# An attention batch on four engines: where the output projection stands on TensorE, and where ScalarE makes queries and keys

## What is computed

```python
qkv = (x @ Wqkv.T + bqkv).reshape(Bb, Ss, 3, H, HD).transpose(2, 0, 3, 1, 4)
attn = jax.nn.softmax(jnp.einsum('bhid,bhjd->bhij', q, k) / jnp.sqrt(jnp.float32(HD)), axis=-1)
coh = jax.nn.sigmoid(jnp.tanh(comb @ Wc1.T + bc1) @ Wc2.T + bc2).transpose(0, 2, 1)
mod = attn * coh[..., None]
mod = mod / (mod.sum(-1, keepdims=True) + 1e-08)
mod = (1.0 - fi) * mod + fi * fa[:, None, :, None]
out = jnp.einsum('bhij,bhjd->bhid', mod, v).transpose(0, 2, 1, 3).reshape(Bb, Ss, Ee)
return out @ Wout.T + bout
```

## Time and profile before

| | us |
|---|---|
| median of 3 runs | 784.82 |
| the three runs | 787.23, 784.77, 784.82 |
| the profiled execution, its own time | 787.02 |
| its span | 785.2 |
| PE busy in the span | 741.9 |
| ACT busy | 575.6 |
| DVE busy | 557.1 |
| POOL busy | 312.2 |

### The profile page before, as it was taken

How to read it: one execution, slowest core, us unless ns; L and a number is a source line. 1 busy time by engine, 2 the same in 40 slices (tenths; PEclk the granted TensorE clock), 3 DMA queues, 4 the chain that set the end, 5 groups by cost and what they waited for, 6 DMA issues and landing times.

```text
span 785.2 us, 14852 instructions
## 1 busy us (share of the span) xinstructions
PE 741.9 (94%) x5314; PEld 654.1 (83%) x5314; DVE 557.1 (71%) x1495; ACT 575.6 (73%) x1001; POOL 312.2 (40%) x214
## 2 busy tenths in 40 slices
PE   6889998979878999999999999999999999999998
PEld 4666767869766799899989989999898899999887
DVE  4887888477379877976977797688679756833422
ACT  3677777369797778978987886897889788553243
POOL 2122222179977175344717543572645161000000
PEclk9999999989997999999999999999999999999999
DMA  8940000000000000000000000000000000000000
GB/s 313 333 117 2 3 1 2 1 1 1 1 1 1 1 1 8 2 1 2 7 1 2 8 1 1 1 8 1 1 5 4 1 1 8 1 1 8 1 1 8
DMA packets 11160, 16.92 MB, mean 22 GB/s; under 512 B 680, under 2 KB 6992, under 8 KB 10832
## 3 DMA queue, kind: packets, MB, share of 16 engines
q1 hardware_dynamic: 10944, 15.72, 6.2%
q10 hardware_dynamic: 144, 0.26, 0.1%
HBM read 14.93 MB, written 1.05 MB: 20 GB/s over the span
## 4 chain that ended last, share of the span: by engine, by line
PE 85%; DVE 6%; ACT 4%; issue 3%; DMA 1%; SPq 0%; DVEq 0%; ACTq 0%
PE banks L448 79%; PE banks L484 4%; ACT G_both L936 2%; PE banks L695 2%; DVE W_both L1444 1%; DMA region<-in_pA 1%; ACT region L1014 1%; DVE acc L1589 1%; PE banks L512 1%; DVE W_both L1213 0%; DVE HF L1450 0%; ACT region L1020 0%; PE banks L727 0%; DVE pairs L1408 0%; DVE top_keys L1403 0%
## 5 line engine op out<-in xcount | busy, mean ns | idle before, releaser
L390 POOL TENSOR_TENSOR region<-sim 128x1024 f32<-128x1024 f32 x128 | 260.8, 2065 | 100.1 <-DVE top_keys L1401 63.2
L1076 ACT ACTIVATE HF<-banks,lpack 128x256 f32<-128x256 f32 x256 | 105.4, 479 | 55.6 <-PE banks L448 54.6
L1014 ACT ACTIVATE region<-region,neg_thr 128x1024 f32<-128x1024 f32 x128 | 143.8, 1153 | 0.0
L1444 DVE SCALAR_TENSOR_TENSOR W_both<-region,rz_rel,W_both 128x1024 f32<-128x1024 f32 x98 | 138.1, 1409 | 1.7
L448 PE MATMUL banks<-HF,w_sb 128*128 128x256 f32 x512 | 124.7, 388 | 7.7 <-DVE HF L1450 7.6
L448 PEld LDWEIGHTS banks<-f_sb,HF 128*128 128x128 f32 x1024 | 123.7, 192 | 3.4
L1020 ACT ACTIVATE region<-region,dtop 128x1024 f32<-128x1024 f32 x114 | 125.3, 1141 | 0.0
L448 PE MATMUL banks<-f_sb,HF 128*128 128x128 f32 x1024 | 124.5, 275 | 0.0
L448 PE MATMUL banks<-cT,f_sb 128*128 128x256 f32 x512 | 122.7, 382 | 0.1
L448 PEld LDWEIGHTS banks<-HF,w_sb 128*128 128x128 f32 x512 | 95.4, 194 | 20.0 <-DVE HF L1450 8.6
L448 PEld LDWEIGHTS banks<-cT,f_sb 128*128 128x128 f32 x512 | 92.1, 190 | 16.3 <-issue 2.9
(11 more groups left out here) (167 smaller groups left out, 1032.7 us busy)
## 6 DMA issues: line engine op xcount, KB each, us to landing
w_sb<-in_w SPq DMA_DIRECT2D x1, 2048.0 KB, 14.0
f_sb<-in_f SPq DMA_DIRECT2D x1, 2048.0 KB, 15.8
region<-in_wq SPq DMA_DIRECT2D x1, 1024.0 KB, 7.9
region<-in_wqT SPq DMA_DIRECT2D x1, 1024.0 KB, 10.0
w_sb<-in_w SPq DMA_DIRECT2D x1, 1024.0 KB, 8.5
out_x<-acc_f SPq DMA_DIRECT2D x16, 64.0 KB, 1.6
x1T_all<-in_xT SPq DMA_DIRECT2D x1, 768.0 KB, 7.7
region<-in_pA SPq DMA_DIRECT2D x1, 588.5 KB, 6.3
```

Of the source, the lines that this page charges most:

```text
L390: pool.tensor_tensor(S[a][h].rearrange("p (i j) -> p i j", i=NK), sim[a][:, h, :].unsqueeze(2).broadcast_to([P, NK, NK]), sim[a][:, PH + h ...
L1014: act.activation(S[a][h], S[a][h], ACT.Prelu, bias=neg_thr[t % 4][:, h:h + 1], alpha=STEEP).then_inc(h_L, 1)
L1076: m = act.activation(HF[e % 2][:, f, :], bank(2 + b, 256 * (f % 2), 256 * (f % 2) + 256), ACT.Gelu_apprx_tanh, bias=L("bf", 4 * e + f, 4 * ...
L1444: v.scalar_tensor_tensor(W[a], S[a][h], rz_rel[a][:, h:h + 1], W[a], ALU.mult, ALU.add).then_inc(h_w, 1)
```

## The change

On TensorE, `out_proj(b - 1)` is no longer issued between the fourth and the fifth of the second transposes of b, but behind the eighth, ahead of `project(b + 2)`. On ScalarE, `queries_keys(b + 2)` is no longer issued between the two exponentials of b+1, but ahead of `keep_values(b)`; its order against out_x1 of b-1, which precedes it, stays.

```diff
@@ transposes(b, q), TensorE @@
                 for g in range(8):
                     m = pe.transpose(bank(g // FG, P * (g % FG), P * (g % FG) + P), D[q][:, P * g:P * g + P], A("ident"))
-                    if g == 3 and q == 1 and b > 0:
-                        out_proj(b - 1)
                 m.then_inc(s_T, 1)
@@ attend, TensorE @@
                 transposes(b, 1)
+                if not first:
+                    out_proj(b - 1)
                 if first:
                     setup_done("fpT")
@@ attend, ScalarE @@
+                if project_more:
+                    queries_keys(b + 2)
                 keep_values(b)
                 if more:
                     exps(b + 1, 0)
-                if project_more:
-                    queries_keys(b + 2)
-                if more:
                     exps(b + 1, 1)
```

## The result

The changed kernel took 776.04 us (median of 6 runs, 774.66 to 778.08) against 784.8 (median of 6, 784.51 to 787.23). The medians are 8.8 us apart; the ratio of the runs is 0.9875, 95% interval 0.986 to 0.989, which is 9.8 us (8.6 to 11.0) of 784.8. The forecast was 775.3 and a saving of 9.5.

What follows compares the result with a forecast made beforehand. TensorE's chain, with one ScalarE copy, was taken to bound the kernel; afterwards VectorE loops at 7.06 per batch. Savings of 9.57 and 0.40 make 9.97, less 0.5: 9.5, so 784.8 becomes 775.3 us; 8-in-10 range 773.6 to 779.6.

Steps and rivals of the forecast that it cites:

- The gap before scores is late keys: Between first transposes and scores: 0.30 us of issue gap per batch comes from GpSimd finishing head_keys late, and goes.
- Output projection: Behind the second transposes: transposes to copy falls from 1.58 to 1.08 us, the projection hidden under that copy.
- Without this cover it would cost 0.22: The moved projection's two TensorE passes would cost 0.22 us if the copy of the transposed probabilities did not hide them.
- Queries and keys: On ScalarE ahead of keep_values: their wait costs nothing; from second transposes, keep_values ends at 3.45, first transposes start at 4.68.
- What is late next: After the edit VectorE, by way of ScalarE, bounds each batch: two loops of 7.06 us, TensorE's own 6.89.
- DVE L1213 in the chain of every batch: Expected sign: VectorE's second subtraction appears in the printed chain of waits in every batch.
- The second transposes released by L936: Expected sign: TensorE's second transposes wait for ScalarE's first copy, L936.
- Sum over the batches: Second transposes of batch 14 come 9.57 us earlier, 0.40 more to batch 15's subtraction, then 0: 9.97.
- The allowance of 0.5: Taken off the 9.97 us: 0.04 per batch for waiting among three loops within 0.17 of each other.
- L1220 beside head_keys costs 0: VectorE's copy from a bank would not be slowed by GpSimd's head_keys, which it now overlaps.
- The slower rival: GpSimd's head_keys hold L1220 and its values add holds L1213: 0.55 us more per batch, 791 us; chance 0.03.
- Clock: Rival: shifted work adds or drops a half-clock stretch on TensorE, the run groups 2.4 us apart; 777.7 us; chance 0.15.

Runs made afterwards that it cites:

- projection-only kernel: The changed kernel with queries and keys back in their old place, so only the output projection moved; ratio 0.9939 to the kernel before.
- keys-only kernel: The kernel before with queries and keys ahead of keep_values, the projection still between the transposes; ratio 0.9925 to the kernel before.
- the one with the keys behind keep_values: The changed kernel with queries and keys one place later, between keep_values and the first exponential; ratio 0.9924 to the kernel before.

## Why the prediction was right, point by point

- *The gap before scores is late keys:* shown. It is there in the projection-only kernel (0.30) and gone in the keys-only kernel and in the changed one.
- *Output projection:* transposes to copy 1.08 forecast, 1.10 measured; values at 2.25, measured 2.27; hidden, shown by doubling it. "Without this cover it would cost 0.22" was not tested as such.
- *Queries and keys:* keep_values ends at 3.45, measured 66.88+0.38-63.91 = 3.35; first transposes 4.68, measured 4.70; scores 5.65, measured 5.67.
- *What is late next:* period 7.06, measured 7.07, and the loop was shown by adding to VectorE (all exposed) and to TensorE (0.16 to 0.19 free). ACT's idle before the second exponential: 0.6 forecast, 0.70 measured. Two of the signs failed. "DVE L1213 in the chain of every batch": the chain prints TensorE alone, since its busy time closes almost every gap. "The second transposes released by L936": printed only once (0.17 at 34.59), since TensorE fills that wait with the output transpose. With more work on VectorE it is printed (0.22).
- *Sum over the batches:* batch 1 was held at 28.44 and came at 27.36, for a reason other than the edit; from there, batch 2 7.22, measured 7.23; batch 3 8.27, measured 8.12, since the small operation behind the key scaling (L1281) had also been stretched and I had counted only the 0.88 of the two large ones; batch 1 to 14 93.15, measured 93.08; to the subtraction of batch 15 0.40, measured 0.38; in batch 15 0, and the step from subtraction to transposes is equal (4.83).
- *The allowance of 0.5:* mis-sized. The loops interlock with no visible loss (every period 7.06 or 7.07). Without it the forecast would have been 774.8; the ratio makes it 775.0. The median, 776.04, is 1.2 above 774.8; that the allowance brought the forecast nearer to it is luck.
- *L1220 beside head_keys costs 0:* it takes 0.41 beside them (67.33, with head_keys from 66.97). L1212 beside head_keys and values takes 1.22. The slower rival did not happen, though its mechanism exists: it is cden, not the copy, that GpSimd can hold: its head_keys in the kernel with late keys, its values in the one with the keys behind keep_values.
- *Clock:* the rival's 2.4 us did not show in the saving. Full clock instead of half in batch 15 made 1.45 of the difference between the two profiled executions, and that belongs to neither order.

The two halves alone save 4.8 and 5.9 by their ratios, 10.7 together against 9.8, which is equal within the intervals. By the period they save 0.27 (mean of the two) and 0.38, together 0.65 of 0.70: nearly additive. Part of this is chance: cden's stall takes from the projection alone what the whole change avoids. Without the stall (7.28) it saves 0.49, and the two would then add up to more than the whole, since VectorE's loops stop the gain at 7.06.

## What to carry to other kernels

Write out the loops between engines, from one event to the same event of the next turn, before trusting a chain of waits: here the chain named TensorE, and a loop over VectorE and ScalarE with 0.17 more was the real bound, to 0.01 us. Take each term from a row without a wait in it; a row that contains one (1.58 with 0.16 of waiting) is right for the kernel at hand and wrong for a changed one. Work put into a wait that exists anyway is free, and how much of the wait is left can be measured by doubling the work in place.

## What was unexpected of the hardware

A VectorE scalar operation of 16 elements, SBUF to SBUF, took 0.93 instead of 0.16 when GpSimd's 1.04 us multiplication had begun 0.15 before it, and ended with it; when it began 0.01 earlier it took 0.16 and GpSimd 1.05. So a difference of 0.16 in start made 0.77 in length. The copy and the subtraction out of a bank, and a reciprocal of 16 elements from SBUF to SBUF, were not touched (0.41, 1.22 and 0.25 beside the same instruction).
